# Latent attention on Trainium2: heads laid out in strips of 32 rows by DMA, scores of four strips side by side, the causal mask added by TensorE

## The reference, cut to what matters

```python
cq, ckv = gelu(x @ wq + bq), gelu(x @ wkv + bkv)            # 64 latent columns each
q = gelu(concat([cq @ wqc + bqc, rope(x @ wqr + bqr)]))     # 128 + 128 columns = 16 heads of 16
k = gelu(concat([ckv @ wkc + bkc, rope(x @ wkr + bkr)]))
v = ckv @ wv + bv
scores = einsum('bhqd,bhkd->bhqk', q, k) / sqrt(16)         # per item and head 112 x 112
scores = where(causal, -inf, scores)
out = softmax(scores) @ v                                   # heads put together again
x = layernorm(x + out @ wo + bo)
```

## Time and profile before

| | us |
|---|---|
| median of three runs (1238.16 to 1244.15) | 1242.25 |
| the profiled execution | 1239.79 |
| its span | 1238.0 |
| latent attention, first block | 733.7 to 753.5 |
| latent attention, second block | 753.6 to 897.3 |
| granted TensorE clock over the span, 1 = 2.4 GHz | 0.901 |

### The profile page before, as it was taken

How to read it: one execution, slowest core, us unless ns; L and a number is a source line. 1 busy time by engine, 2 the same in 40 slices (tenths; PEclk the granted TensorE clock), 3 DMA queues, 4 the chain that set the end, 5 groups by cost and what they waited for, 6 DMA issues and landing times. The chain is left out here.

```text
span 1238.0 us, 17895 instructions
## 1 busy us (share of the span) xinstructions
PE 1069.1 (86%) x6426; PEld 802.0 (65%) x6426; DVE 622.6 (50%) x1350; ACT 394.2 (32%) x996; POOL 171.9 (14%) x178
## 2 busy tenths in 40 slices
PE   7667757999999999869999977777789999999884
PEld 4455545787778777669999953334376677766642
DVE  2555444555555555656555544676524444444314
ACT  2323331333333333334454413333323222222100
POOL 0222205011101100013333304221010000000000
PEclk9788868999999999979999987777799999999865
DMA  4400000000000000063210000000000000000001
GB/s 136 147 8 7 0 25 27 12 14 13 12 2 0 0 0 0 1 221 96 69 34 34 1 1 1 1 1 0 1 25 13 13 14 13 13 25 1 1 0 30
DMA packets 23959, 31.34 MB, mean 25 GB/s; under 512 B 5009, under 2 KB 19570, under 8 KB 23906
## 3 DMA queue, kind: packets, MB, share of 16 engines
q1 hardware_dynamic: 23906, 30.64, 7.8%
HBM read 29.71 MB, written 0.92 MB: 25 GB/s over the span
## 5 line engine op out<-in xcount | busy, mean ns | idle before, releaser
L1020 ACT ACTIVATE x_prob<-bank,x_negmax 112x375 f32<-112x375 f32 x128 | 72.3, 570 | 151.5 <-DVE x_negmax L935 151.5
L1696 POOL TENSOR_TENSOR moe_sq<-moe_r 128x448 f32<-128x448 f32 x64 | 64.4, 1008 | 122.2 <-ACT moe_r L1728 102.5
L1655 DVE TENSOR_TENSOR moe_h_low<-moe_sq,moe_h_high 128x448 fp32r<-128x448 f32 x64 | 54.3, 866 | 53.2 <-ACT moe_h_high L1720 38.9
L86 PE MATMUL bank<-moe_w_low,moe_h_high 128*112 128x256 f32 x256 | 71.8, 280 | 0.0
L86 PE MATMUL bank<-moe_w_high,moe_h_high 128*112 128x256 f32 x256 | 71.7, 280 | 0.0
L86 PE MATMUL bank<-moe_w_high,moe_h_low 128*112 128x256 f32 x256 | 71.7, 280 | 0.0
L935 DVE TENSOR_REDUCE x_negmax<-bank 112x1 f32<-112x375 f32 x128 | 64.1, 543 | 7.2 <-PE bank L826 4.9
L1728 ACT ACTIVATE moe_r<-bank 128x448 f32<-128x448 f32 x64 | 34.9, 546 | 86.9 <-PE bank L86 85.4
L940 DVE COPY x_prob_t<-bank 125x336 f32<-125x336 f32 x128 | 59.1, 499 | 6.6 <-PE bank L835 4.7
L847 PEld LDWEIGHTS bank<-x_prob_t,x_v 125*64 125x64 f32 x768 | 37.2, 136 | 33.9 <-issue 29.9
L1421 ACT ACTIVATE x_prob<-bank,x_negmax 112x375 f32<-112x375 f32 x64 | 36.1, 569 | 70.4 <-DVE x_negmax L1336 70.4
(11 more groups left out here) (354 smaller groups left out, 2405.3 us busy)
## 6 DMA issues: line engine op xcount, KB each, us to landing
moe_w<-in_L_ffn_W SPq DMA_DIRECT2D x16, 512.0 KB, 4.6
x_ctx_t<-in_ctx_t SPq DMA_DIRECT2D x16, 376.0 KB, 3.1
wk<-in_L_xattn_Wk SPq DMA_DIRECT2D x2, 1024.0 KB, 6.8
wv<-in_L_xattn_Wv SPq DMA_DIRECT2D x2, 1024.0 KB, 8.9
wq<-in_L_xattn_Wq SPq DMA_DIRECT2D x2, 1024.0 KB, 11.6
wo<-in_L_xattn_Wo SPq DMA_DIRECT2D x2, 1024.0 KB, 13.5
w_in<-in_L_attn_W_in SPq DMA_DIRECT2D x1, 1160.0 KB, 7.1
xt<-in_xt SPq DMA_DIRECT2D x1, 896.0 KB, 4.7
```

Of the source, the lines that this page charges most:

```text
L86: last = pe.matmul(out, lhs, rhs, start=(k == 0), stop=(k == len(pairs) - 1))
L1020: act.activation(PROB(u, e)[:, :], S_BANK(u, e)[0:T, 0:S], ACT.Exp, bias=negmax[:, g:g + 1], accum_out=total[:, g:g + 1]).then_inc(p_ready, 1)
L1655: dve.tensor_tensor(h_low[half][:, m, :], sq[m % 2][:, :], h_high[half][:, m, :].bitcast(F32), ALU.subtract).then_inc(low_done, 1)
L1696: pool.tensor_tensor(sq[m % 2][:, :], r[m % 2][:, :], r[m % 2][:, :], ALU.mult).then_inc(sq_done, 1)
```

## The change

The score matmuls no longer use all 128 rows with zeros in all but 16. Instead q and k are copied once more by DMA, into `q_strips` and `k_strips` of [128, 4, 896]: head h stands in rows 32 * (h // 4) to + 16, at index h % 4; the other 16 rows of each strip are zero (set by POOL at the start of the first block). SP issues these DMAs in the first block, eight for each chunk, each 16 rows of 448 columns: 64 in all. Then a group's four heads lie in one strip, and for each of four indices four matmuls, one in each strip of 32 rows, write four banks. The causal mask is put into a bank before that by a matmul of a bf16 identity with a bf16 tile `hide` that holds the mask four times; the products are added to it.

`scores(i)` now does all four banks at one place in a round, at j == 2 between `weigh(i, 1)` and `out_projection(i - 1)`, waits until all masks of the item before are done, and signals once. DVE's mask has two operations left, both reading the bank. POOL's `round_` is gone, `values` reads `lat` itself, and the loop is written out in full (`overlapped_in_full`).

```diff
+    for i in range(-1, B + 1):
+        round_(i, i % 2, i + 1 < B, 0 <= i < B, i > 0)
...
+                    pool.memset(q_strips[:, :, :], 0.0)
+                    pool.memset(k_strips[:, :, :], 0.0).then_inc(strips_cleared, 1)
+                    pool.wait_ge(strips_cleared, 1)
+                    pool.tensor_copy(hide[:, :, :], core.c(T, C_CAUSAL, T).unsqueeze(1).broadcast_to([T, GB, T]))
+                    pool.tensor_copy(ident_low[:, :], core.c(T, C_ID, T)).then_inc(strips_cleared, 1)
...
+                    def fill(s, strips, grouped, c):
+                        cols = slice(s * HALF, (s + 1) * HALF)
+                        for k in range(2 * GB):
+                            h = 2 * GB * c + k
+                            sp.dma_start(strips[32 * (h // GB):32 * (h // GB) + HD1, h % GB, cols],
+                                         grouped[HD1 * k:HD1 * (k + 1), c, cols]).then_inc(strips_filled[s], 16)
+                    sp.wait_ge(strips_cleared, 1)
+                    for s in range(2):
+                        sp.wait_ge(cont_used, s + 1)
+                        fill(s, q_strips, qg, 0)
+                        fill(s, k_strips, kg, 0)
+                        sp.wait_ge(gelu_done, 2 * s + 1)
+                        fill(s, q_strips, qg, 1)
+                        sp.wait_ge(gelu_done, 2 * s + 2)
+                        fill(s, k_strips, kg, 1)
...
-                        wait_past(pool, s_ready, NG * (i - 1))
-                        for c in range(KD):
-                            pool.tensor_tensor(k_sep[p][:, c, :, :], kg[:, c, bass.ts(i, T)].unsqueeze(1).broadcast_to([128, 8, T]),
-                                               core.c(128, C_HEAD, 8).unsqueeze(2).broadcast_to([128, 8, T]), ALU.mult)
-                        wait_past(pool, v_ready, i - 1)
-                        pool.tensor_copy(lat_i[p][:, :], lat[0:LAT, bass.ts(i, T)])
-                        pool.tensor_copy(q[p][:, :, :], qg[:, :, bass.ts(i, T)]).then_inc(sep_ready, 1)
...
-                    def scores(i, p, j):
-                        if j == 0:
-                            pe.wait_ge(sep_ready, i + 1)
-                        wait_past(pe, s_used, NG * (i - 1) + j + 1 if not isinstance(i, int) or i else 0)
-                        heads = slice(j % 2 * GB, (j % 2 + 1) * GB)
-                        pe.matmul(bank[j][0:T, 0:GB * T], q[p][:, j // 2, :],
-                                  k_sep[p][:, j // 2, heads, :].rearrange("d h t -> d (h t)"), start=True, stop=True).then_inc(s_ready, 1)
+                    def scores(i):
+                        if i % HI == 0:
+                            pe.wait_ge(strips_filled[i // HI], 16 * 4 * 2 * GB)
+                        wait_past(pe, masked_ready, NG * i)
+                        for b in range(NG):
+                            pe.matmul(bank[b][0:T, 0:GB * T], ident_low[:, :], hide[:, :, :].rearrange("t h s -> t (h s)"),
+                                      start=True, stop=False)
+                        item = slice(i * T, (i + 1) * T)
+                        for hh in range(GB):
+                            for b in range(NG):
+                                strip = slice(32 * b, 32 * b + 32)
+                                last = pe.matmul(bank[b][0:T, hh * T:(hh + 1) * T], q_strips[strip, hh, item], k_strips[strip, hh, item],
+                                                 start=False, stop=(hh == GB - 1))
+                        last.then_inc(s_ready, 1)
...
-                            if front and j > 0:
-                                scores(i + 1, 1 - p, j - 1)
+                            if front and j == 2:
+                                scores(i + 1)
...
-                        if front:
-                            scores(i + 1, 1 - p, NG - 1)
...
-                        chain_m.resume(i, 2 * j)
-                        dve.wait_ge(s_ready, NG * i + j + 1)
-                        m = masked[j % 2]
+                        chain_m.resume(i, j)
+                        dve.wait_ge(s_ready, i + 1)
+                        scores = bank[j][0:T, 0:GB * T].rearrange("t (h s) -> t h s", h=GB)
                         t = top[:, GB * j:GB * (j + 1)]
+                        chain_m.link(dve.tensor_reduce(t, scores, AX_X, ALU.max))
                         wait_past(dve, e_done, NG * i + j - 1)
-                        chain_m.link(dve.tensor_tensor(m[:, :, :], bank[j][0:T, 0:GB * T].rearrange("t (h s) -> t h s", h=GB),
-                                                       core.c(T, C_CAUSAL, T).unsqueeze(1).broadcast_to([T, GB, T]), ALU.add))
-                        dve.sem_inc(s_used, 1)
-                        chain_m.link(dve.tensor_reduce(t, m[:, :, :], AX_X, ALU.max))
-                        dve.tensor_tensor(m[:, :, :], m[:, :, :], t.unsqueeze(2).broadcast_to([T, GB, T]),
+                        dve.tensor_tensor(masked[j % 2][:, :, :], scores, t.unsqueeze(2).broadcast_to([T, GB, T]),
                                           ALU.subtract).then_inc(masked_ready, 1)
```

More of the change, by code:

```diff
@@ L152, in overlapped, with overlapped_in_full @@
     round_(B, 0, False, False, True)
+def overlapped_in_full(round_):
+    for i in range(-1, B + 1):
+        round_(i, i % 2, i + 1 < B, 0 <= i < B, i > 0)
 def nothing(item, p):
@@ L1870, in latent_attention @@
         qg, kg = sbw("qg", [128, KD, N]), sbw("kg", [128, KD, N])
+        q_strips, k_strips = sbw("q_strips", [128, NG, N]), sbw("k_strips", [128, NG, N])
+        hide = whole.enter_context(nc.sbuf_tensor("la_hide", [T, GB, T], BF16))
+        ident_low = whole.enter_context(nc.sbuf_tensor("la_ident", [T, T], BF16))
         wv, wo, rows = core.la_wv, core.la_wo, core.la_rows
@@ L1873, in latent_attention @@
         wo_loaded = core.wo_loaded
+        strips_cleared, strips_filled = sem("strips_cleared"), [sem("strips_filled0"), sem("strips_filled1")]
         with ExitStack() as ctx:
@@ L1887, in latent_attention, with _ @@
             with nc.Block() as block:
+                @block.gpsimd
+                def _(pool):
+                    pool.memset(q_strips[:, :, :], 0.0)
[3 more added lines that the diff above has]
+                    pool.tensor_copy(ident_low[:, :], core.c(T, C_ID, T)).then_inc(strips_cleared, 1)
+                @block.sync
+                def _(sp):
+                    def fill(s, strips, grouped, c):
[13 more added lines that the diff above has]
+                        fill(s, k_strips, kg, 1)
                 @block.tensor
@@ L1943, in latent_attention @@
             pair = lambda name, shape: [sb(f"{name}{p}", shape) for p in range(2)]
-            q, k_sep, lat_i = pair("q", [128, KD, T]), pair("k_sep", [128, KD, 8, T]), pair("lat_i", [LAT, T])
             v = pair("v", [T, H1, AUG])
@@ L1985, in _ @@
                     last.then_inc(ones_set, 1)
-                    overlapped(pool, round_)
                 @block.tensor
@@ L1990, in _ @@
                     ident = core.c(128, C_ID, 128)
-                    def scores(i, p, j):
-                        if j == 0:
-                            pe.wait_ge(sep_ready, i + 1)
-                        wait_past(pe, s_used, NG * (i - 1) + j + 1 if not isinstance(i, int) or i else 0)
-                        heads = slice(j % 2 * GB, (j % 2 + 1) * GB)
-                        pe.matmul(bank[j][0:T, 0:GB * T], q[p][:, j // 2, :],
-                                  k_sep[p][:, j // 2, heads, :].rearrange("d h t -> d (h t)"), start=True, stop=True).then_inc(s_ready, 1)
+                    def scores(i):
[12 more added lines that the diff above has]
+                        last.then_inc(s_ready, 1)
                     def values(i, p):
                         wait_past(pe, nt_copied, i - 1)
-                        pe.matmul(bank[4][0:T, 0:D], lat_i[p][:, :], wv[:, :], start=True, stop=True).then_inc(v_ready, 1)
+                        pe.matmul(bank[4][0:T, 0:D], lat[0:LAT, i * T:(i + 1) * T], wv[:, :], start=True, stop=True).then_inc(v_ready, 1)
                     def turn(i, j):
@@ L2070, in _ @@
                     pe.wait_ge(wo_loaded, 48)
-                    overlapped(pe, round_)
+                    overlapped_in_full(round_)
                 @block.vector
                 def _(dve):
-                    chain_m, chain_d, chain_e = Chain(dve, mask_chain, 2 * NG), Chain(dve, divide_chain, 1), Chain(dve, end_chain, 5)
+                    chain_m, chain_d, chain_e = Chain(dve, mask_chain, NG), Chain(dve, divide_chain, 1), Chain(dve, end_chain, 5)
                     def add_bias(i, p):
@@ L2139, in _ @@
                     dve.wait_ge(wo_loaded, 48)
-                    overlapped(dve, round_)
+                    overlapped_in_full(round_)
                 @block.scalar
@@ L2190, in round_ @@
                             copy_state(i - 1)
-                    overlapped(act, round_)
+                    overlapped_in_full(round_)
 def build(nc, d, out):
```

10 lines of the change are left out of this document (3 added, 7 removed).

## The result

The changed kernel takes 1262.11 us (median of 4 runs, 1258.21 to 1264.17), the kernel before 1241.72 beside it: a ratio of 1.016, with a 95% interval of 1.0129 to 1.0191. The forecast was 1242, from 1230 to 1258. The profiled execution took 1258.21 us, its span is 1256.3, and its granted clock 0.884 (before 0.901).

A forecast was written before the change was run, and what follows sets the result against it. The prediction took the cycle of waits within a round, no engine being full, to bound the kernel. Copies +23.1, rounds -15.7 and start -7.6 gave -0.2 on 1239.8, so 1239.6; with 2.4 for the median, 1242.0 us, range 1230 to 1258.

The forecast's parts named there:

- the copies: SP's 64 DMA issues in the projections' block delay its barrier: second block at 776.6 against 753.57, +23.1 us.
- the rounds: Six full rounds of the latent attention loop: 83.7 us against 99.45, -15.7 (ends -26 and -3.5).
- The term 0.51 us for an issue: SP's queue in the first block: each strip copy's issue takes 0.51 us, from two issues 1.02 us start to start.
- The upper bound of 0.64: SP's queue: dearest case for one issue, midway to the heavy weight-load row, making the barrier delay +31.4 us.
- X: Block after `weigh(i, 1)`: four mask matmuls and 16 strip products, 2.1 us at full clock, 3.6 at half.
- round 6's clock: Loop: with the earlier sixth round's clock (full from 868.87) a new round takes 13.1 us; with round 5's, 14.8.
- near 0.7: Sign expected in the profile after: PE's granted clock in the loop near 0.7.
- Rival 4: Loop: with the long scores gone PE stays at half clock, round 16.0, +12 us, 1254; chance 0.15.
- POOL: Loop: POOL leaves; its four rounds were 2.5 us longer on average, a gain counted in the base rounds.
- The mask: Round: four mask matmuls on PE, 0.8 to 1.6 us at full clock, 1.6 to 3.2 at half; DVE's mask 1.97 to 1.2.
- the start: Second block's opening to the first `turn_output`: +18.4 us in place of +25.98, -7.6 (bounds -6 and -9).
- rival 5: Strip products run in turn, not side by side: +2.5 to 3 us a round, +18, 1260; chance 0.13.

The follow-up runs named there:

- the six groups above: Kernel before plus 48 unread copies issued by SP beside its rounds, eight per group, differing in source and size: 1239.9 us in a single execution.
- The filled run: Changed kernel plus unread fp32 products of 112 columns in PE's pauses in a round: 1239.19 us, ratio 0.997 to the kernel before.
- the round of 17.81 us above: A round of the changed kernel with heads 16 rows deep (8 copies), mask on PE and unread products in PE's pauses: kernel 1217.32 us.
- the two last runs: Changed kernel with 8 copies, unread products in pauses and at the first block's end: mask on PE 1201.97 us; mask on DVE, doubled filling, 1205.46 us.
- the filled start: Changed kernel with 8 copies and filled pauses, plus sixteen unread products at the first block's end and four behind the first values: 1201.97 us, ratio 0.9683.

## Why the prediction was wrong, by its own steps

The median missed by 20.1 us. In the profiled executions the copies were 8.1 us dearer than forecast and the rounds gained 9.9 less. Most of the rest is that the changed kernel's median lies 3.9 us above its profiled execution, where the prediction added 2.4.

**The copies: mechanism right, size off.** Forecast +23.1, measured +31.2. The barrier includes the issues, the first issue (743.57 against 743.75) and the 64 in a row came as said. The term 0.51 us for an issue measured 0.634, 7.9 us in all. Every row it was taken from the earlier trace rows was a transfer from HBM, and the calm-queue reasoning treated a copy from SBUF as the same thing; the six groups above show that it isn't. The upper bound of 0.64 held by luck: it was taken midway to the row of a heavy transfer. The prediction also gives 28 KB as the size of the transfer with 0.47 on the queue; that row moves 8.0 KB, and 28 KB is a strip copy.

**The rounds: the step that failed.** Forecast -15.7, measured -5.8. All parts but X are within some 0.1 us of the forecast for a half-clock round, and X is 0.3 shorter. In the fastest round X starts 4.2 us into the round (4.1), takes 3.26 (3.6), then 0.95 (0.86), 1.17 (1.16), 1.74 (1.75) and 3.36 (3.3); together 14.69 (14.8). The step that failed is the sentence that half of the rounds would have round 6's clock, full from X on, at 13.1 us. None had: in all six X starts at half. Four of six rounds are of the 14.7 to 15.6 kind, and two are 16.7 and 17.0, half until the projection is over. Over the six the granted clock is 0.69 on average, the "near 0.7" that the prediction gave as its sign, so the mean clock of a loop does not tell the length of its rounds. I took the clock of two rounds that belong to another order of work. The filled run shows how much hangs on it: with the same order of work, and added products that only lengthen PE's queue, rounds go from 15.6 us on average to 12.0 where the clock is full. Within one kernel, with the same products in each round, 16.33 and 12.03 us stand side by side.

The Trainium skill (TensorE: Matmul & The Clock Gate, A second HAM failure mode: psum-queue depth-cycling) describes a clock that alternates between its levels because PE idles briefly and often between groups of products. The changed kernel's trace agrees: pauses of 0.29 to 1.19 us, two levels within each round. It is not the whole cause: the round of 17.81 us above, with PE busy for 17.30, stayed at 0.50. Why the clock rises where it does stays open.

**Rival 4** (clock at half, round 16.0, 1254) is nearest to what happened, though the rounds were 15.6 us and their clock 0.60 to 0.77, not 0.5. With 7.9 us for the issues it gives 1262; that it meets the measured median to the us is luck, since its round is 0.4 us too long. I had 0.15 on it and 0.64 for an issue as a bound, and left the two together out of the range, though neither depends on the other.

**POOL.** Its 2.5 us a round were counted in the base rounds. It does leave, and the copy of x is 0.29 us in every round. With POOL's work back, four rounds wait 1.07 to 1.15 us for the stretched DVE. In the old order the 2.5 us shrink where the clock is nearly equal: round 3 with POOL takes 17.29 us at 0.80 (814.67 to 831.96) and round 5 without it 15.36 at 0.79, 1.9 less; with the pauses filled it is 17.14 at 0.80 (rounds 2 to 4) and 15.85 at 0.79 (5 and 6), 1.3 less. The rest comes from round 6, whose clock was 0.88.

**The mask.** Left inside X. The forecast of its size was good at full clock (0.90 measured from 837.36 to 838.26, forecast 0.8 to 1.6) and at half (1.67, forecast 1.5 to 3.2). The prediction asked too little whether the other side gains: DVE's shorter mask was off the path, as it found itself ("`values` ends at 877.88"), so PE paid for nothing. I expected 7 us from undoing it, and the profiles show 8.3. That is at a clock of 0.6 to 0.75; the two last runs show no such gain at full clock, with the filling changed as well. The prediction calls mask, strips and projection three modes; by their shapes (112, 32 and 128 rows deep) only the strips use groups of rows, and PE shows no idle time between the three.

**Right:** the start (-7.4, forecast -7.6), the tail (0), the strips side by side (32 passes in 1.59 us, so rival 5 is out), the covered wait of X for the masks (DVE's last mask of the item ends at 882.53, X starts at 884.78), and nothing seen for the unrolling, which no run isolates.

## What to carry to other kernels

Price a DMA issue from a row with the same source and count every issue inside a block that ends in a barrier: 64 small copies cost 31 us where 8 larger ones cost 4. Where TensorE's clock moves between its levels, a round's length at one clock says nothing about a changed round; work the sum at both, and try cheap unread products in the pauses before judging the order of work: here that turned 1.6% slower into 0.3% faster, with fewer copies into 2%, and with the filled start into 3%. In the kernel before they gave 0.2%: where PE waits for another engine, a faster PE gains little. A saving on one engine is worth its price on another only if the first is late.

## What was not expected of the hardware

- In groups of eight, an issue on SP's queue takes 0.63 us from SBUF for 1 and for 16 rows and 0.75 for 112 rows, and 0.45 to 0.46 from HBM for 16 and for 128 rows.
- The same round of work takes 12.03 us at a granted clock of 1.00 and 17.8 at 0.50. Adding 11% to PE's products (99 to 110 in a round) made the changed kernel's rounds shorter.
- After PE had stood still for 4.5 us, the clock stayed at half for 49 us in which PE was busy for all but some 2.1 (758.90 to 808.00). What lets it rise stays open: added products raised it in the changed order (0.60 to 0.77 became 0.75 to 1.00) and not in the last two rounds of the old one (0.79 and 0.88 became 0.79 twice).
- Heads 16 rows deep run side by side too: four groups of eight passes start 0.19 to 0.29 us apart at full clock, masks and strips together taking 1.88 us (816.16 to 818.04).
- VectorE's copy goes from 0.29 to 1.53 us beside GpSimd, and in the changed order 1.07 to 1.15 us of that reach TensorE at the start of four rounds.
